# Mask and maxima in one product, maxima moved through memory, and 128 stationary columns in every tile of the second scores

## The reference, cut to what matters

```python
q, k, v = heads(ln(x) @ Wq + bq), heads(ctx @ Wk + bk), heads(ctx @ Wv + bv)
scores = einsum('bhqd,bhkd->bhqk', q, k) / sqrt(16)
scores = where(mask, -1e15, scores)
attn = softmax(scores, axis=-1)
x = x + tanh(g_xattn) * (merge(attn @ v) @ Wo + bo)
w, i = top3(softmax(tanh(mean(ln(x)) @ W1 + b1) @ W2 + b2))     # per batch
x = x + tanh(g_ffn) * (ln(x) + sum_k w[k] * gelu(ln(x) @ Wa[i[k]]) @ Wb[i[k]])
```

## Time and profile before

| | |
|---|---|
| median of 3 runs | 368.09 us (367.42 to 371.11) |
| the profiled execution | 368.46 us |
| its span in the profile | 366.7 us, 1.8 us less than its time |
| busy: PE, DVE, ACT, POOL | 88%, 55%, 53%, 43% |

### The profile page before, as it was taken

The page is one execution under the profiler, slowest core; times in us unless marked ns, Lnnn a source line. Parts: engine busy times, 40 slices in busy tenths (PEclk is TensorE's granted clock), DMA queues, the critical chain, the costliest instruction groups (busy, mean ns, idle before and its releaser), DMA issues.

```text
span 366.7 us, 10035 instructions
## 1 busy us (share of the span) xinstructions
PE 321.9 (88%) x3732; PEld 269.1 (73%) x3732; DVE 202.9 (55%) x607; ACT 194.7 (53%) x398; POOL 159.4 (43%) x219
## 2 busy tenths in 40 slices
PE   1766899799799998999999878579889999999996
PEld 1543576576576776767777556479889999999996
DVE  4335457367267477575675944266555555455452
ACT  3244366565565765665667567344446545554442
POOL 4863866458559569576598868200100000000000
PEclk9958699999899999999999999699999999999999
DMA  8956847748547658556376414010101011011000
GB/s 176 271 142 179 213 124 193 158 129 212 134 132 188 163 133 238 165 154 184 83 198 168 146 54 118 17 39 2 45 22 39 6 37 39 4 39 35 7 14 13
DMA packets 32927, 40.47 MB, mean 110 GB/s; under 512 B 9993, under 2 KB 26689, under 8 KB 32881
## 3 DMA queue, kind: packets, MB, share of 16 engines
q1 hardware_dynamic: 26176, 22.07, 23.4%
q0 software_dynamic: 4784, 16.98, 16.4%
q10 hardware_dynamic: 1920, 0.79, 0.9%
HBM read 33.09 MB, written 6.74 MB: 109 GB/s over the span
## 4 chain that ended last, share of the span: by engine, by line
PE 65%; POOL 9%; DMA 7%; DVE 7%; issue 5%; ACT 4%; DVEq 1%; SPq 0%; ACTq 0%; POOLq 0%
PE bank L1182 15%; PE bank L1201 15%; PE bank L1031 6%; PE bank L1039 5%; PE bank L979 4%; POOL wa L447 4%; PE bank L989 4%; DMA stage<-in_L_ffn_Wa 3%; PE bank L1013 3%; PE bank L999 3%; PE bank L993 3%; PE bank L1056 2%; DMA stage<-in_L_ffn_Wb 2%; DVE bank L741 2%; POOL stage L442 2%
## 5 line engine op out<-in xcount | busy, mean ns | idle before, releaser
L741 DVE CUSTOM_DVE_ANT_0 bank<-bank,maskb 112x375 f32<-112x375 f32 x128 | 67.7, 568 | 37.5 <-PE bank L979 37.2
L1182 PE MATMUL bank<-ctxT,wqkvo 128*128 128x112 f16 x960 | 61.4, 216 | 10.5 <-DVE qbd L909 10.5
L1182 PEld LDWEIGHTS bank<-ctxT,wqkvo 128*128 128x128 f16 x960 | 59.0, 100 | 12.1 <-issue 11.8
L1201 PE MATMUL bank<-wb,stage 128*112 x576 | 66.8, 273 | 0.0
L1201 PEld LDWEIGHTS bank<-wb,stage 128*112 128x112 f16 x576 | 62.3, 130 | 0.2
L529 ACT ACTIVATE pT<-bank 125x448 f32<-125x448 f32 x96 | 48.9, 540 | 19.5 <-PE bank L999 19.3
L706 ACT ACTIVATE kst<-bank 128x448 f32<-128x448 f32 x48 | 25.7, 535 | 57.4 <-PE bank L1182 57.4
L447 POOL TENSOR_TENSOR wa<-stage,wa 128x512 f16<-128x512 f32 x32 | 36.7, 1158 | 23.8 <-ACT wa L628 23.6
L908 DVE COPY wqkvo<-wa 128x3072 f16 x24 | 23.2, 966 | 43.1 <-PE bank L1182 38.3
L442 POOL TENSOR_SCALAR stage<-stage 128x512 f32<-128x512 f32 x64 | 39.3, 625 | 15.5 <-DMA stage<-in_L_ffn_Wa 9.2
L979 PE MATMUL bank<-kst,qbd 128*112 128x375 f16 x128 | 36.6, 349 | 10.6 <-DVE peaks L741 7.0
(11 more groups left out here) (115 smaller groups left out, 467.4 us busy)
## 6 DMA issues: line engine op xcount, KB each, us to landing
stage<-in_L_ffn_Wa POOLq DMA_DIRECT2D x16, 512.0 KB, 5.1
stage<-in_L_ffn_Wb POOLq DMA_DIRECT2D x16, 512.0 KB, 4.9
kst<-k_scr SPq DMA_DIRECT2D x64, 93.8 KB, 3.9
k_scr<-k_hl SPq DMA_DIRECT2D x16, 187.5 KB
ctx_s<-in_ctx SPq DMA_DIRECT2D x8, 336.0 KB
qbd<-q_scr SPq DMA_DIRECT2D x32, 56.0 KB, 3.2
xa<-in_x SPq DMA_DIRECT2D x8, 112.0 KB, 2.3
q_scr<-q_hl SPq DMA_DIRECT2D x32, 28.0 KB
```

The source lines that it names most:

```text
L741: v.tensor_tensor_reduce(out=bank[0:SQ, e, 0:SK], in0=bank[0:SQ, e, 0:SK], in1=maskb[:, b % 2, 0:SK], scale=-1.0, scalar=3.0e38, op0=ALU.a ...
L1182: ins = T.matmul(o, first(ws, t, f), x2b[:, b % 2, (xs * DT + t) * SQ:(xs * DT + t + 1) * SQ], start=(t == 0 and xs == 0 and ws == 0), sto ...
L1201: ins = T.matmul(o, hT[:, u % 2, hs * FT * SQ + f * SQ:hs * FT * SQ + (f + 1) * SQ], wb[:, bass.ds(e * (4 * CHUNK) + ws * (2 * CHUNK) + f ...
```

## The change

- The mask's product of `st_tile` gets three more rows of contraction: `rq` holds an identity in its first 112 rows and the three parts of the maxima in rows 112 to 114, against rows of ones in `maskb`. The four products of line 999 and the tensors `pick` and `ident_b` are gone.
- The maxima cannot be written into three partitions in that layout by an engine; they go out to memory (`write_max`, twice for each batch) and come back (`move_max`, four times for each batch, into one of two halves of `rq`). The first tile of each couple waits for that DMA (`rq_in`).
- The third chunk's tiles use 128 stationary columns too (they were 125), with padding in `kst` and `maskb`. Masked scores are held at a floor, and a row 125 of the third chunk in `pT` and `vp` (the context's sum, scaled by 2^-100, summed by the two `cx_copy`) gives the mean value where a query's keys are all masked.
- The order is another one: `s1` of batch `b + 1` starts in slot 0 of `b` (it was slot 1, and its last pair slot 0 of the next `b`); `MX0`, `MX1` stand inside slot 2 and slot 0; `K0`, `K1` come before `Q`; `mask_bias` runs in slot 3. VectorE fills three more regions at the start, ahead of TensorE's first product.

```diff
--- before.py
+++ after.py
     n, m, o = b + 1, b + 2, b - 1
     every = (
-        (("V0", n), ("XT", m), ("V1", n), ("MX1", b), ("CX0", m), ("CX1", m)),
-        (("Q", m), ("OT", o), ("K0", m), ("K1", m), ("X2T", b - 2)),
-        (("ON", o),),
-        (("MX0", n), ("OP", o)),
+        (("MX1", b), ("V0", n), ("XT", m), ("V1", n), ("CX0", m), ("CX1", m)),
+        (("K0", m), ("K1", m), ("Q", m), ("OT", o), ("X2T", b - 2)),
+        (("MX0", n), ("ON", o)),
+        (("OP", o),),
...
-        ident_b = sb("ident_b", [SQ, SQ], BF16)
-        pick = sb("pick", [128, 4, 128], BF16)
+        rq = sb("rq", [KQ, 2, QUAD], BF16)
...
-        kst = sb("kst", [128, 2, PAIRS * SK], F16)
+        kst = sb("kst", [128, 2, PAIRS * SK + 4], F16)
         qbd = sb("qbd", [128, 2, 2, PAIRS, SQ], F16)
-        vp = sb("vp", [CK, 2, KC, NH, VC])
-        pT = sb("pT", [CK, PRING, QUAD])
+        vp = sb("vp", [CK + 1, 2, KC, NH, VC])
+        pT = sb("pT", [CK + 1, PRING, QUAD])
         mask_s = sb("mask_s", [SQ, SK], U8)
-        maskb = sb("maskb", [SQ, 2, SK], BF16)
-        ms = sb("ms", [128, COUPLES, SQ], BF16)
-        peaks = sb("peaks", [SQ, COUPLES, 5, 4])
+        maskb = sb("maskb", [KQ, 2, SK + 4], BF16)
+        ms = sb("ms", [12, 2, SQ], BF16)
+        peaks = sb("peaks", [SQ, COUPLES, 4, 4])
...
+            def write_max(b, h):
+                if there(b):
+                    sp.wait_ge(s["ms_done"], 2 * b + h + 1)
+                    sp.dma_start(m_scr[b, h, :, :, :], ms[:, :, :]).then_inc(s["m_written"], 16)
+
+            def move_max(b, g):
+
+                if there(b):
+                    sp.wait_ge(s["m_written"], 16 * (2 * b + g // 2 + 1))
+                    need(sp, s["pe_st"], tile(b, g, 0) - KC)
+                    sp.dma_start(rq[SQ:KQ, g % 2, :].rearrange("c (j q) -> c j q", j=4),
+                                 m_scr[b, g // 2, :, g % 2, :].rearrange("(c j) q -> c j q", j=4)).then_inc(rq_in[g % 2], 16)
...
+                move_max(b, 1)
                 read_q(n, 1)
                 read_k(n, 1)
+                write_max(b, 1)
                 load_xr(o)
                 load_mask(m)
                 load_x(m + 1)
-
                 load_ctx(m + 1)
-                write_q(m)
-                store_r(b - 2)
-
+                move_max(b, 2)
                 write_k(m, 0)
                 write_k(m, 1)
-                store_x2(b - 2)
+                move_max(b, 3)
+                write_q(m)
+                write_max(n, 0)
...
+                read_k(m, 0)
+                move_max(n, 0)
                 read_q(m, 0)
-                read_k(m, 0)
+                store_r(b - 2)
+                store_x2(b - 2)
...
-            chain.link(g.tensor_copy(ident_b[:, :], ident[0:SQ, 0:SQ]))
+            g.tensor_copy(rq[0:SQ, :, :].rearrange("p i (j f) -> p (i j) f", f=SQ),
+                          bass.AP(ident, 0, [[128, SQ], [0, 8], [1, SQ]])).then_inc(s["rq_ready"], 1)
             chain.link(g.memset(one[:, :], 1.0))
-            chain.link(g.memset(ms[:].rearrange("p a f -> p (a f)"), 0.0))
-            chain.link(g.memset(pick[:].rearrange("p a f -> p (a f)"), 0.0))
-            for c in range(3):
-                ins = g.affine_select(out=pick[:, :, :], in_=pick[:, :, :], compare_op=ALU.not_equal, fill=1.0,
-                                      base=-4 * c, pattern=[[-1, 4], [0, 128]], channel_multiplier=1)
-                if c < 2:
-                    chain.link(ins)
-            ins.then_inc(s["pick_ready"], 1)
+            chain.link(g.memset(vsc[:, :], 1.0))
+            g.affine_select(out=vsc[:, :], in_=vsc[:, :], compare_op=ALU.not_equal, fill=TINY,
+                            base=-CK, pattern=[[0, 1]], channel_multiplier=1).then_inc(s["ones_ready"], 1)
+            pool.wait_ge(s["zeroed"], 6)
+            sums = vp[:, :, KC - 1, :, HD]
+            g.affine_select(out=sums, in_=sums, compare_op=ALU.not_equal, fill=SK * TINY,
+                            base=-CK, pattern=[[0, 2], [0, NH]], channel_multiplier=1).then_inc(s["ones_ready"], 1)
...
-                    c, n = ((0, 2), (2, 1))[half_]
+                    c, n, rows_ = ((0, 2, CK), (2, 1, CK + 1))[half_]
                     at = (b % 2) * (KC * NH * VC) + c * (NH * VC)
-                    a.activation(bass.AP(vp, at, [[2 * KC * NH * VC, CK], [VC, n * NH], [1, HD]]),
-                                 spare_bank(name)[0:CK, 0:n * D].rearrange("p (h i) -> p h i", i=HD), ACT.Copy).then_inc(s["v_done"], 1)
+                    if b == 0:
+                        act.wait_ge(s["ones_ready"], 2)
+                    a.activation(bass.AP(vp, at, [[2 * KC * NH * VC, rows_], [VC, n * NH], [1, HD]]),
+                                 spare_bank(name)[0:rows_, 0:n * D].rearrange("p (h i) -> p h i", i=HD), ACT.Copy,
+                                 scale=vsc[0:rows_, :]).then_inc(s["v_done"], 1)
...
-                    need(act, s["pe_st"], tile(b - 1, 2 * h + 2, 0))
-                    a.activation(ms[0:12, 2 * h:2 * h + 2, :].rearrange("r c q -> r (c q)"),
+                    need(act, s["m_written"], 16 * (2 * b + h))
+                    a.activation(ms[0:12, :, :].rearrange("r c q -> r (c q)"),
                                  spare_bank(name).bitcast(BF16)[0:12, 0:2 * SQ], ACT.Copy).then_inc(s["ms_done"], 1)
...
-                    a.activation(ctxT[:, 0, :], spare_bank(name)[:, 0:SK], ACT.Copy).then_inc(s["cx0_done"], 1)
+                    a.activation(ctxT[:, 0, 0:SK], spare_bank(name)[:, 0:SK], ACT.Copy, accum_out=ctxT[:, 0, SK:SK + 1]).then_inc(s["cx0_done"], 1)
...
                 exp_tile(b, 0, 0)
                 exp_tile(b, 0, 1)
+                max_copy(b, 1)
                 o_copy(o)
                 exp_tile(b, 0, 2)
-                mask_bias(n)
                 v_copy(n, 0)
                 xt_copy(m)
                 v_copy(n, 1)
-                max_copy(b, 1)
...
-                q_hi(m)
                 k_hi(m, 0)
                 k_hi(m, 1)
+                q_hi(m)
...
                 exp_tile(b, 2, 1)
+                max_copy(n, 0)
                 exp_tile(b, 2, 2)
...
-                max_copy(n, 0)
+                mask_bias(m)
...
+            v.memset(maskb[:, :, :], 1.0).then_inc(s["zeroed"], 1)
+            v.memset(kst[:, :, PAIRS * SK:PAIRS * SK + 4], 0.0).then_inc(s["zeroed"], 1)
+            v.memset(pT[96:CK + 1, :, :], 1.0).then_inc(s["zeroed"], 1)
+            dve.wait_ge(s["zeroed"], 6)
             for b in range(-2, B):
                 n, m, o = b + 1, b + 2, b - 1
-                row_max(b, 6)
-                row_max(b, 7)
-                split_max(b, 1)
+                row_max(n, 0)
+                row_max(n, 1)
                 cx_copy(m)
                 if b == B - 1:
                     route_logits(0)
 
-                row_max(n, 0)
-                row_max(n, 1)
-                if b == -2:
-                    dve.wait_ge(s["wq_scaled"], 2)
-                q_lo(m)
-                o_rows(o)
-                if b == -2:
-                    dve.wait_ge(s["bk_loaded"], 16)
-                k_lo(m, 0)
-                result(b - 2)
-                k_lo(m, 1)
-                if b == B - 1:
-                    route_top(0)
-
                 row_max(n, 2)
                 row_max(n, 3)
                 split_max(n, 0)
+                if b == -2:
+                    dve.wait_ge(s["wq_scaled"], 2)
+                    dve.wait_ge(s["bk_loaded"], 16)
+                k_lo(m, 0)
+                k_lo(m, 1)
+                q_lo(m)
+                o_rows(o)
+                result(b - 2)
+                if b == B - 1:
+                    route_top(0)
+
+                row_max(n, 4)
+                row_max(n, 5)
                 x2_lo(b - 2)
                 ln1_stats(m + 1)
 
-                row_max(n, 4)
-                row_max(n, 5)
+                row_max(n, 6)
+                row_max(n, 7)
+                split_max(n, 1)
...
-                    w = 128 if c < KC - 1 else CK
-                    T.matmul(o[0:w, :].rearrange("k (j q) -> k j q", j=4), maskb[:, b % 2, c * CK:c * CK + w],
-                             bass.AP(ident_b, 0, [[SQ, SQ], [0, 4], [1, SQ]]), start=True, stop=False)
+                    if c == 0:
+                        pe.wait_ge(rq_in[g % 2], 16 * (2 * b + g // 2 + 1))
+                    T.matmul(o, maskb[0:KQ, b % 2, c * CK:c * CK + 128], rq[0:KQ, g % 2, :], start=True, stop=False)
                     for i in range(2):
                         p = 2 * g + i
-                        T.matmul(o[0:w, i * 2 * SQ:(i + 1) * 2 * SQ].rearrange("k (e q) -> k e q", e=2),
-                                 kst[:, b % 2, p * SK + c * CK:p * SK + c * CK + w], qbd[:, b % 2, :, p, :],
-                                 start=False, stop=False)
-                    if c == 0:
-                        pe.wait_ge(s["ms_done"], 2 * b + g // 2 + 1)
-                    for j in range(4):
```

(21 more changed lines are left out.)

64 lines of the change are left out of this document (40 added, 24 removed).

## The result

The changed kernel takes 393.85 us (median; 391.12 to 395.94) against 368.47 of the kernel before in the same comparison: a ratio of 1.072, 95% interval 1.067 to 1.077. I had predicted 369.0 us, which is no change, with a range of 359 to 377. The kernel is 7.2% slower, and the prediction was wrong. Some executions of a kernel are slower than the others; the medians here take in all of them and the ratios leave those out, which matters most for e10_onchip_reduce, where nine of twelve are left out and the other three have a median of 364.0 us.

What follows compares the result with a forecast made beforehand. The prediction took TensorE and a second loop, the weights' loop through GpSimd, as the bound, with the new memory path equally long at 23.6 us a period. Sum: 368.5 + 7.6 - 5.0 + 0.9 - 2.6 = 369.4, so 369.0 us; range 359 to 377.

Steps and rivals of the forecast that it cites:

- Head: Start, up to `w_hi` of slot 1: fills, q ready last, `V0` to `CX1` no longer hidden; +7.6 us, shift stays.
- five periods: Slot 1 of `b` = 0 to slot 1 of `b` = 5: 1.0 us saved per period, -5.0 us, bounds -8.5 to +2.5.
- the sixth: `b` = 5 to `b` = 6: no weights' loop in slot 0, memory path sets `V0` at T + 20.0; +0.9 us.
- the end: Loop's end: GpSimd's wait for `w_hi` in slot 0 of `b` = 7 goes; -2.6 us, bounds -3.5 and -1.
- the zones: The part after the loop over `b`, not touched by the change: 0 +- 0.5 us.
- The weights' loop: `w_hi` of slot 1, GpSimd, `normed`, exponential, tile: 11.96 us whatever TensorE does; holds the period at 23.6 us.
- The new memory path: Maxima and q through memory to slot 0's scores at T + 17.7; period 23.6 us, no cost beyond the weights' loop.
- s1 to V0: TensorE's work in slot 0 from the awaited scores at T + 17.7 to `V0`: 2.3 us.
- C: Rival: SyncE's queue is the bound, `move_max(n, 0)` waiting ahead of the q reads; period 24.9, 376.8 us; chance 17%.
- A: Rival: TensorE alone is the bound, so all 21.8 us come off; 346.7 us; chance 4%.
- B: Rival: the head is cheap and the memory path quick, bounds on the good side; 360.6 us; chance 22%.
- D: Rival: VectorE's `result` line is held up by GpSimd's `lo_part`, delaying slots 2 and 3; 372.3 us; chance 7%.

Runs made afterwards that it cites:

- e10_onchip_reduce: e9_onchip with VectorE's one copy of the maxima parts replaced by two reductions; 367.6 us, ratio 0.989 to the kernel before.
- e13_before_whi: Kernel before the change, with the two `w_hi` of slot 1 moved ahead of the copies of k on ScalarE; 361.7 us, ratio 0.982.
- e12_onchip_whi: e10_onchip_reduce with the two `w_hi` of slot 1 moved ahead of the copies of k; 358.5 us, ratio 0.973 to the kernel before.
- e8_no_crowd: Changed kernel with most loads of the zones' weights cut to 8 of 1024 columns, same instructions, queues and waits; 372.8 us, ratio 1.007 to the kernel before.
- e1_order_only: Changed kernel with new order, sums and 128 columns, but maxima added by four products, not through memory; 384.1 us, ratio 1.038 to the kernel before.
- e3_warm: Changed kernel plus 18 extra products ahead of TensorE's wait for the maxima in slot 0; 385.1 us, ratio 1.046 to the kernel before.
- e9_onchip: Kernel before with one product for mask and maxima, 128 columns, maxima moved by transposes and a ScalarE copy, order kept; 385.1 us, ratio 1.041.

## Why the prediction was wrong, step by step

*The terms.* Head +10.5 us (7.6 predicted), five periods +10.3 (-5.0), the sixth +6.2 (+0.9), the end -1.6 (-2.6), the zones -0.8 (0). Most of the error, 15.3 us, is in the five periods.

*The weights' loop*: right. 10.88 us from `w_hi` to `normed` before and after, and moving `w_hi` alone gives 1.8% (e13_before_whi). It is one reason why 21.8 us of TensorE's products can't be had for the asking, and not the only one: with `w_hi` moved in both kernels, the removed products, less what 12 more transposes a batch cost, are worth 3.1 us. In `b` = 2 to 4 TensorE waits 1.17 us for VectorE's row maxima ahead of a pair of `s1` in e12_onchip_whi, 0.44 in e13_before_whi.

*The new memory path*: this step failed, and with it the claim that its wait costs nothing beyond the weights' loop. I had the scores of slot 0 at T + 17.7 and `V0` 2.3 us behind; they are at T + 20.2 and 3.9 us. Of the 2.5 us, 0.8 came before the write of the maxima was out (0.76 us for `move_max(b, 3)`, which I had not counted ahead of the q writes, is nearly all of it), 1.15 from its landing, 3.75 us for 5 KB where I took 2.6 from a write of 112 KB, 0.35 from the move's issue (0.75, not 0.4), the rest in between; the q reads landed in 3.3 us, as I took it. I took a median over the run; what counts is the landing at that place, where the weights' load of 512 KB is under way (e8_no_crowd). And I did not put q's own write to memory on the path: in every other batch of e1_order_only it lands 4.2 to 5.5 us after its issue has ended, and alone holds the scores to T + 19.5 to 19.7. With it, "the memory path is as long as the weights' loop" could not have stood.

*V0 to slot 1*: 3.44 us, I had 3.6. *s1 to V0*: the second failed term, 3.9 us where I had 2.3, since I costed it at full clock. I had seen half clock behind a wait at the head and used it there, but not here, though I forecast a wait of 2 us in every batch. e3_warm prices it: 1.5 us a period, 8.8 us in all. 2.5 + 1.6 - 0.2 is 3.9 us, my 23.6 against 27.5.

*From `b` = 5 to `b` = 6*: +6.2 against +0.9. 4.5 of it are the same two errors: scores at T + 20.15, `V0` 4.3 us behind. The rest came behind them: the twelve products of `V` took 3.71 us, before 2.75.

*The head*: +8.4 at `w_hi` of slot 1 (7.6 predicted); the fills cost 1.7, not 0.5 (first product 9.27 against 7.59), the first scores came 2.1 later and not 3. That the shift stays was wrong: the waits of slot 0 (2.2 for the maxima, 0.9 for q) made it 10.5 by slot 1 of `b` = 0.

*The end*: -1.6 (predicted -2.6, within its bounds), GpSimd's wait is gone. *The zones*: -0.8, just outside my 0.5.

*The rivals.* C had the place and the mechanism: the queue behind `move_max(n, 0)`. Its price was too low (scores at T + 19.0, period 24.9): a larger landing for the write of the maxima and the clock were missing. A and B had no part. D happened in part: line 848 (`result`) ran 0.89 us or more in all six of its runs inside the loop, against 0.48 twice in the zones. Four of the six took 0.89 to 0.90 us, one 0.98, and one 2.13 (228.89, `b` = 6), with a wait of TensorE of 2.2 us for the row maxima behind it. In the studied batch the 0.4 us were hidden under the wait for memory. Its mechanism, VectorE held by GpSimd, is also the one that cost e9_onchip 17.5 us. One reading of mine was too neat: six of the seven short ones of before ran while GpSimd was idle, but the one at 220.31 began inside a `lo_part` (219.31 to 220.48) and still took 0.47 us.

```profile
L848 DVE SCALAR_TENSOR_TENSOR xr<-x,tgate,xr x8: 479/894/2131, 120.5 to 289.3; 112x256 f32<-112x256 f32 x8
```

*The Trainium skill.* I had weighed the Trainium skill's page "DMA: Bandwidth & Descriptors", whose section on the anatomy of one DMA puts a fixed cost of some 2.0 us on each. That section describes a DMA that GpSimd issues, which I had passed over; those of this path are issued by SyncE. The reads in e8_no_crowd (2.2 us) are near it; the write of 5 KB in the full kernel (3.75 us) is not. The measurement decides: beside 512 KB loads it is no estimate for a path of several landings.

What stays open is how the 14 us that the new order costs without the maxima's trip split between the place of q and of the scores: no run moved one of the two alone. By the slots of the profiled execution of e1_order_only (16.3 us longer in the span than before) they are 9.6 us in the head, 2.5 in the five periods and 4.2 behind them. So in the head nearly all of the loss is the order; in the five periods 7.8 of the 10.3 us come with the maxima's trip.

## What to carry to other kernels

When a change puts data on a path through memory, write down every landing on it, the first write's too, and take each from rows at that moment of the loop, beside the loads that run then, not from a median. Where the forecast has TensorE wait, cost what stands behind the wait at the lower clock, or fill the wait with products. And when a saving stays away, shorten the other loop first: one move of two instructions gave 1.8%, the removed products, 21.8 us of TensorE's time, at best about 1% each time.

## What the runs showed of the hardware

- A write of 5 KB landed 2.9 to 5.3 us after its issue began in the batches of the changed kernel; q's writes landed 2.5 to 5.5 us after the end of their issue in e1_order_only.
- The move of the 2.6 KB takes 0.75 us of the queue's time to issue, an x load of 112 KB 0.31.
- 18 useless products ahead of a wait made the changed kernel 2% faster (385.1 us against 393.9): the granted clock stayed at 1.00 where it had been 0.65.
- A VectorE instruction with both inputs in SBUF, 0.48 us by itself, took 0.89 to 2.13 us in the changed kernel's loop, the longest beside two of GpSimd's `lo_part` (228.47 to 230.73).
- A VectorE copy of 112 x 24 bf16 elements took 0.19 to 3.40 us; a reduction of half of them 0.19 to 0.21 us.
